# A routed feed-forward layer that sorts tokens into expert tiles through DRAM, and a shorter start of the delta attention

## The reference, cut to what matters

```python
def _L3_ffn_ref(x, Ws1, bs1, Ws2, bs2, We1, be1, We2, be2, Wr, br):
    D, E, HS, HR, TAU = 128, 12, 256, 384, 1.5
    xf = x.reshape(-1, Dm)                                   # 2048 tokens
    ys = _geglu(xf @ Ws1 + bs1) @ Ws2 + bs2                  # shared expert
    logits = (xf @ Wr + br) / TAU
    top_val, top_idx = jax.lax.top_k(logits, 2)
    top_w = jax.nn.softmax(top_val, axis=-1)
    onehot = jax.nn.one_hot(top_idx, E, dtype=x.dtype)
    w = jnp.einsum('nke,nk->ne', onehot, top_w)              # 2 of 12 nonzero
    act = _geglu(jnp.einsum('nd,edh->enh', xf, We1) + be1[:, None, :])
    yE = jnp.einsum('enh,ehd->end', act, We2) + be2[:, None, :]
    yr = jnp.einsum('end,ne->nd', yE, w)
    return (ys + yr).reshape(B, T, Dm)
```

## Time and profile before

| | |
|---|---|
| median of three runs | 3347.52 us (3342.79 to 3354.88) |
| the profiled execution's own time | 3348.08 us |
| its span in the profile | 3346.3 us, at a mean granted TensorE clock of 0.878 |
| busy: PE, DVE, ACT, POOL | 2732.6, 2249.3, 1317.0, 375.6 us |
| DMA | 213.99 MB, 64 GB/s on the mean |

### The profile page before, as it was taken

The page is one execution under the profiler, slowest core; times in us unless marked ns, Lnnn a source line. Parts: engine busy times, 40 slices in busy tenths (PEclk is TensorE's granted clock), DMA queues, the critical chain, the costliest instruction groups (busy, mean ns, idle before and its releaser), DMA issues. The chain is left out here.

```text
span 3346.3 us, 65597 instructions
## 1 busy us (share of the span) xinstructions
PE 2732.6 (82%) x25488; PEld 1777.4 (53%) x25488; DVE 2249.3 (67%) x3961; ACT 1317.0 (39%) x2809; POOL 375.6 (11%) x348
## 2 busy tenths in 40 slices
PE   6777887788778887799399999986775777699998
PEld 5677777777667776633166666632221222244443
DVE  4999999999999999700367778825665666422222
ACT  2233333333333333322367777741113454522223
POOL 0000000000000000000310110002330111044443
PEclk8788788788887778899699999997887899899999
DMA  4111111111111111110499999610001111211000
GB/s 157 27 28 27 27 28 27 27 27 27 27 27 27 27 27 27 36 25 0 109 228 243 238 230 248 158 47 2 0 0 41 46 43 37 96 36 31 31 31 31
DMA packets 194794, 213.99 MB, mean 64 GB/s; under 512 B 29842, under 2 KB 175650, under 8 KB 189138
## 3 DMA queue, kind: packets, MB, share of 16 engines
q1 hardware_dynamic: 194529, 210.03, 23.7%
HBM read 142.71 MB, written 67.03 MB: 63 GB/s over the span
## 5 line engine op out<-in xcount | busy, mean ns | idle before, releaser
L576 DVE SCALAR_TENSOR_TENSOR rf_A<-ps,rf_bias,rf_G 128x512 f32<-128x512 f32 x152 | 114.1, 751 | 275.2 <-POOL rf_G L558 260.6
L2364 DVE TENSOR_REDUCE dl_ZO<-dl_XP 128x64 f32<-128x128 f32 (+6 forms) x448 | 219.6, 490 | 15.4
L1104 DVE TENSOR_REDUCE ra_top<-ps 128x1 f32<-128x512 f32 x256 | 161.3, 683 | 94.7 <-PE ps L908 94.4
L547 ACT ACTIVATE rf_G<-ps,rf_bias 128x512 f32<-128x512 f32 x152 | 104.4, 687 | 287.8 <-PE ps L528 287.8
L558 POOL TENSOR_TENSOR rf_G<-rf_G,rf_WB 128x512 f32<-128x512 f32 x144 | 182.2, 1265 | 272.2 <-ACT rf_G L547 272.2
L2046 PE MATMUL ps<-dl_kqN,dl_ST 64*64 64x32 f32 x4224 | 195.3, 265 | 17.2 <-DVE dl_ST L2387 17.2
L2360 DVE TENSOR_TENSOR dl_XP<-dl_ZO,dl_G 128x64 f32<-128x64 f32 (+6 forms) x448 | 194.5, 434 | 15.4
L2046 PEld LDWEIGHTS ps<-dl_kqN,dl_ST 64*64 64x64 f32 x4224 | 192.5, 191 | 19.8 <-issue 19.7
L1303 POOL MEMSET da_K<- 32x4096 f32 x2 | 7.2, 3576 | 1607.6 <-POOLq L82 1607.6
L1758 DVE TENSOR_TENSOR ps<-ps,da_window 128x192 f32<-128x192 f32 (+1 forms) x256 | 101.2, 395 | 122.2 <-PE ps L1487 117.7
L1761 DVE TENSOR_REDUCE da_top<-ps 128x1 f32<-128x512 f32 x256 | 177.0, 691 | 8.8
(11 more groups left out here) (352 smaller groups left out, 6106.8 us busy)
## 6 DMA issues: line engine op xcount, KB each, us to landing
da_bands<-da_AB SPq DMA_DIRECT2D x128, 384.0 KB, 3.8
dl_Abc<-dl_ends SPq DMA_DIRECT2D x64, 512.0 KB, 6.2
da_window<-da_bands SPq DMA_DIRECT2D x128, 192.0 KB, 4.4
da_across<-da_bands SPq DMA_DIRECT2D x128, 192.0 KB, 4.4
rf_WB<-rf_shares SPq DMA_DIRECT2D x48, 256.0 KB, 3.2
da_parts<-da_split SPq DMA_DIRECT2D x64, 96.0 KB, 3.3
rf_We<-in_rf_We SPq DMA_DIRECT2D x1, 4608.0 KB, 15.9
da_K<-da_parts SPq DMA_DIRECT2D x16, 256.0 KB
```

Of the source, the lines that this page charges most:

```text
L1104: eng.tensor_reduce(top[:, m % 2, u:u + 1], ps[:, score_bank(UNITS * m + u), :], AXX, ALU.max, negate=True).then_inc(s["maxima"], 1)
L2364: link(eng.tensor_reduce(ZO[:, to:to + 1 + (2 * I - 1) * CH:CH].rearrange("p (k i) -> p k i", k=2), XP[:, :, :, SB - 1 - t:], AXX, ALU.add))
```

## The change

**Routed layer.** One block takes the place of two. After the top-2 chain, two matmuls with a strictly triangular matrix and with a matrix of ones count for each token how many tokens before it go to the same expert. DVE works these counts into a row number for each of the 4096 (token, choice) pairs: the rows of an expert are together and start at a multiple of 128. This gives SLOTS = 43 tiles of 128 rows (32 would hold 4096 rows; the rest is room for 12 experts that do not fill their last tile). The tiles run whether or not they hold rows.

- PE turns X into token-major tiles, ACT copies each of them twice to `XT`; a 129th column holds the row number to return to.
- SP fills all 43 x 128 rows of a DRAM array `rf_slots` with zeros and default row numbers (2.84 MB, rows of 516 B). POOL then **scatters** `XT` into it with 32 indirect DMAs of 128 rows. SP fetches it back in 11 DMAs of four tiles, one after the other.
- Meanwhile PE, ACT and DVE compute the shared expert and the term with be2 (28 matmuls of 512 columns) into R.
- **The tile loop**, written out 43 times: PE transposes the tile, DVE copies it to SBUF; DVE loads the tile's expert number into a register and copies the expert's first weights (128x768) to a fixed place `W1`, PE does 3 gate and 3 up matmuls of 128 columns, ACT 3 gelus, DVE 3 products, PE loads the same number into a register of its own and does 3 second matmuls with a register as address, ACT copies the result, POOL scatters it with an indirect DMA of 128 rows to the row (2 x token + choice) of `rf_results`.
- At the end SP loads the results of each batch (512 KB) one after the other, DVE weights and adds the two choices of each token, PE transposes the sum, DVE adds it to R.

**Delta layer.** PE starts the k projections as soon as the k taps are there, not those of q; the four `start(0, r)` on the zero state are left out, as is the transpose of `begin(0, 0)`, and `empty_state()` puts zeros and bv in place; DVE does both `prepare` before `gate_keys(0)`. The layer's semaphores are given back when the fifth layer begins, since the last layer needs 34.

The diff, cut to its core:

```diff
-            @block.sync
-            def _(eng):
-                eng.wait_ge(weights_c, B)
-                eng.dma_start(shares, WT[0:E, :, :]).then_inc(loaded, 16)
...
+        @block.sync
+        def _(eng):
+            eng.wait_ge(s["blank"], 1)
+            eng.wait_ge(s["marked"], 3)
+            eng.dma_start(slots.rearrange("(j p) x -> p j x", p=P), XS[:, :, :]).then_inc(s["filled"], 16)
+            eng.wait_ge(s["scattered"], 16 * 2 * NT)
+            for i, (first, last) in enumerate(FETCH):
+                if i:
+                    eng.wait_ge(s["fetched"], 16 * i)
+                eng.dma_start(XS[:, first:last, :], slots[first * P:last * P, :].rearrange("(j p) x -> p j x", p=P)).then_inc(s["fetched"], 16)
+            eng.wait_ge(s["returned"], 16 * SLOTS)
+            for b in range(B):
...
+                eng.dma_start(YT[:, span, :, :].rearrange("p t k x -> p t (k x)"),
+                              results[2 * b * T:2 * (b + 1) * T, :].rearrange("(t p k) x -> p t (k x)", p=P, k=2)).then_inc(s["gathered"], 16)
...
+        @block.gpsimd
+        def _(eng):
+            eng.memset(XS[:, :, 0:P], 0.0)
+            eng.memset(WT[:, :, :], 0.0).then_inc(s["blank"], 1)
+            eng.wait_ge(s["filled"], 16)
+            eng.wait_ge(s["x_copied"], 2 * B)
+            eng.wait_ge(s["marked"], 3)
+            eng.wait_ge(s["chain"], PLACED)
+            for k in range(2):
+                for t in range(NT):
+                    eng.indirect_dma_start(slots, bass.IndirectOffsetOnAxis(rows[:, k, t:t + 1], 0), XT[:, k, t, :], None)\
+                       .then_inc(s["scattered"], 16)
+            for j in range(SLOTS):
+                eng.wait_ge(s["fetched"], 16 * (j // 4 + 1))
+                eng.wait_ge(s["kept"], j + 1)
+                eng.indirect_dma_start(results, bass.IndirectOffsetOnAxis(XS[:, j, P:ROW].bitcast(U32), 0), Y[:, j, :], None)\
+                   .then_inc(s["returned"], 16)
...
+        @block.tensor
+        def _(eng):
...
+            def first(j):
+                eng.wait_ge(s["taken"], j + 1)
+                eng.wait_ge(s["brought"], j + 1)
+                if j >= 2:
+                    eng.wait_ge(s["tile_gelus"], j - 1)
+                    eng.wait_ge(s["tile_acts"], j - 1)
+                for m in range(HR):
+                    mm = eng.matmul(ps[:, 2 + j % 2, m * P:(m + 1) * P], W1[:, j % 2, (HR + m) * P:(HR + m + 1) * P], x[:, j % 3, :],
                                     start=True, stop=True)
+                mm.then_inc(s["gates"], 1)
...
+            def second(j):
+                e = eng.value_load(owners[0:1, j:j + 1], min_val=0, max_val=E - 1)
+                eng.wait_ge(s["tile_acts"], j + 1)
+                if j >= 2:
+                    eng.wait_ge(s["kept"], j - 1)
+                for m in range(HR):
+                    mm = eng.matmul(ps[:, 6 + j % 2, 0:P], A[:, j % 2, m, :], We2[:, bass.ds(e * (HR * P) + m * P, P)],
+                                    start=m == 0, stop=m == HR - 1)
+                mm.then_inc(s["outs"], 1)
...
+            for j in range(SLOTS):
+                if j + 2 < SLOTS:
+                    turn(j + 2)
+                if j + 1 < SLOTS:
+                    first(j + 1)
+                second(j)
...
+        @block.scalar
...
+            eng.wait_ge(s["chain"], OFFSET)
+            gelu(0)
+            for j in range(SLOTS):
+                if j + 1 < SLOTS:
+                    gelu(j + 1)
+                eng.wait_ge(s["outs"], j + 1)
+                eng.activation(Y[:, j, :], ps[:, 6 + j % 2, 0:P], ACT.Copy).then_inc(s["kept"], 1)
 
         @block.vector
...
+            step(eng.tensor_tensor(picked, passed[:, :, :].unsqueeze(2).to_broadcast([P, SLOTS, 2 * HR, E]),
+                                   own_bias.unsqueeze(1).to_broadcast([P, SLOTS, 2 * HR, E]), ALU.mult))
+            step(eng.tensor_reduce(offset[:, :, :], picked, AXX, ALU.add))
...
+            def bring(j):
+                e = eng.value_load(owners[0:1, j:j + 1], min_val=0, max_val=E - 1)
+                if j >= 2:
+                    eng.wait_ge(s["ups"], j - 1)
+                eng.tensor_copy(W1[:, j % 2, :], We1[:, bass.ds(e * (2 * HR * P), 2 * HR * P)]).then_inc(s["brought"], 1)
...
+            for j in range(SLOTS):
+                eng.wait_ge(s["ups"], j + 1)
+                eng.wait_ge(s["tile_gelus"], j + 1)
+                if j >= 2:
+                    eng.wait_ge(s["outs"], j - 1)
+                for m in range(HR):
+                    ins = eng.scalar_tensor_tensor(A[:, j % 2, m, :], ps[:, 4 + j % 2, m * P:(m + 1) * P], offset[:, j, m:m + 1], G[:, j % 2, m, :],
+                                                   ALU.add, ALU.mult)
+                ins.then_inc(s["tile_acts"], 1)
+                if j + 2 < SLOTS:
+                    bring(j + 2)
+                    take(j + 2)
...
             project(0, 2, 4, False)
+            eng.wait_ge(s["prepared"], 3)
+            project(0, 4, 6, False)
             eng.wait_ge(s["prepared"], 4)
-            project(0, 4, PROJ, False)
+            project(0, 6, PROJ, False)
...
-            for r in range(GR):
-                start(0, r)
+            eng.sem_inc(s["y"], GR)
...
+            def empty_state():
+                eng.memset(Y[:, CH:, :], 0.0).then_inc(s["begun"], 1)
+                eng.memset(XP[:, 1, :, 0:SB], 0.0).then_inc(s["begun"], 1)
+                eng.tensor_copy(XP[:, 0, :, 1:][:, :, ::-1], bv[:, 0, :, 0:SB]).then_inc(s["chain"], 1)
...
-            eng.wait_ge(s["prepared"], 4)
...
-            gate_keys(0)
             prepare(0, 0)
             prepare(0, 1)
-            begin(0, 0)
+            empty_state()
+            eng.wait_ge(s["prepared"], 4)
+            gate_keys(0)
             one_pass(0, True)
```

More of the change, by code:

```diff
@@ L487, in routed_ffn @@
-        experts = [(HR, E > 0)] * E + [(HS, False)]
-        before = [sum(h for h, _ in experts[:e]) for e in range(E + 2)]
-        HB = before[E + 1]
-        FREE = HR + 1
+        each = c.sb("rf_each", [P, E, NT], ctx)
+        upto = c.sb("rf_upto", [P, E, NT], ctx)
+        over = c.sb("rf_over", [P, E, NT], ctx)
+        count = c.sb("rf_count", [P, E], ctx)
+        ends = c.sb("rf_ends", [P, E], ctx)
+        begins = c.sb("rf_begins", [P, E], ctx)
+        place = c.sb("rf_place", [P, E, NT], ctx)
@@ new lines, in _ @@
+            eng.wait_ge(s["chain"], ROUTED)
+            flat = both[:, :, :].rearrange("p t e -> p (t e)")
+            eng.matmul(ps[:, 5, 0:NT * E], below[:, :], flat, start=True, stop=True)
+            eng.matmul(ps[:, 6, 0:NT * E], everyone[:, :], flat, start=True, stop=True).then_inc(s["prefixes"], 1)
+            eng.wait_ge(s["chain"], ROUTED + 2)
+            eng.wait_ge(s["x_copied"], 2 * B)
+            for t in range(NT):
+                mm = eng.transpose(ps[0:E, 1 + t // 4, (t % 4) * P:(t % 4 + 1) * P], weights[:, t, :], c.ident[:, :])
+                if t % 4 == 3:
+                    mm.then_inc(s["weights_turned"], 1)
@@ new lines, in _ @@
+            eng.wait_ge(s["weights_copied"], B)
+            eng.wait_ge(s["chain"], PLACED)
+            shared_first(0)
+            for b in range(B):
+                if b + 1 < B:
+                    shared_first(b + 1)
+                shared_second(b)
+            eng.wait_ge(s["base"], B)
+            eng.wait_ge(s["experts_loaded"], 16 * len(large))
+            eng.wait_ge(s["chain"], NAMED)
+            turn(0)
+            turn(1)
+            first(0)
+            for j in range(SLOTS):
[4 more added lines that the diff above has]
+                second(j)
@@ new lines, in _ @@
+            assert steps[0] == PLACED
+            per_slot = [P, SLOTS, E]
+            step(eng.tensor_tensor(passed[:, :, :], numbers[:, :].unsqueeze(2).to_broadcast(per_slot),
+                                   ends[:, :].unsqueeze(1).to_broadcast(per_slot), ALU.is_ge))
+            step(eng.tensor_reduce(owner[:, :], passed[:, :, :], AXX, ALU.add))
+            step(eng.tensor_scalar(owner[:, :], owner[:, :], float(E - 1), None, ALU.min))
+            step(eng.tensor_copy(owners[:, :], owner[:, :]))
@@ L583, in rwkv_attention @@
+            for b in range(B):
+                eng.wait_ge(s["back"], b + 1)
+                eng.tensor_tensor(c.R[:, b, :], c.R[:, b, :], ps[:, b, :], ALU.add)
 def rwkv_attention(c):
```

368 lines of the change are left out of this document (224 added, 144 removed).

## The result

The changed kernel takes 3100.46 us, the median of four runs (3093.74 to 3108.88), against 3350.18 for the kernel before in the same comparison: a ratio of 0.926, interval 0.923 to 0.929. The prediction said 3167 (3085 to 3275). The sign and the range held; the gain is 250 us where 181 were forecast.

The account below looks back on a forecast made before the run. TensorE's columns were taken to bound the last layer's loop, a waiting chain the delta prologue. Gains of 159 us in the last layer and 22 in the first took 3348.1 to 3167 us; range 3085 to 3275, with 0.8 inside.

Parts of the forecast that it names:

- the forecast as described: Whole kernel: the main case without the rivals, a total of 3110 to 3205 us, chance 0.54.
- the tile loop's 3.5 us a tile: Last layer's tile loop: 43 turns of 3.5 us, 150 us in all, bounds 2.5 and 5.5 a tile.
- PE 2.3: Tile loop: nine matmuls of 128 columns and a transpose take TensorE 2.3 us a tile at full clock.
- DVE 2.8, with 1 us for the register load: Tile loop: DVE's products and copies 1.7 to 2.2 us, plus a partly hidden 1 us register load, 2.8 a tile.
- 2.3 / 0.76 is 3.0, and PE's own load and semaphores come on it: Tile loop: TensorE's 2.3 us divided by the recurrence's granted clock, plus load and semaphores, taken as 3.5 a tile.
- the chain over two tiles: Tile loop: gates, gelus, products, load and copy, take and six hand-overs, 5.0 us over two tiles, 2.5 a tile.
- The half clock: Rival, PE in the tile loop: TensorE at 1.2 GHz, 5 us a tile, total 3210 to 3232, chance 0.13.
- The rival of slow ones: Rival, POOL's queue: slow indirect DMAs, total crossing 3348 at 5.1 us each, 3419 at 6; chance 0.11 for slower.
- its middle case: POOL's queue: an indirect DMA between 3 and 4.5 us, total 3215 to 3306, still faster; chance 0.11.
- 2.15 us each: Scatter: if all of a GpSimd DMA held POOL, 32 take 69 us and the total is 21 us more.
- 14 and 2 of landing: Fill of the slots: 14 us behind the large loads plus 2 of landing, so the scatter starts at 2935.
- All cheap: Rival, last layer: indirect DMA 0.45 us, register load 0.3, loop from 2963 at 2.5 a tile, total 3097, chance 0.08.

Follow-up runs that it names:

- run 7: Changed kernel with each register load of the tile loop done three times, on DVE and on PE: 3136.29 us, ratio 0.9355.
- run 4: Changed kernel with no register loads in the tile loop, every tile taking expert 0's weights by fixed addresses: 3100.19 us, ratio 0.927.
- run 6: Changed kernel with two more DVE copies of 128x512 in each turn of the tile loop, into an unread buffer: 3103.13 us, ratio 0.9273.
- run 8: Changed kernel with 32 more indirect DMAs of 64 rows each ahead of the scatter, POOL waiting for them: 3138.63 us, ratio 0.9387.
- run 9: Changed kernel with the two large weight loads issued after the fill on the same queue: 3104.51 us, ratio 0.9263.
- run 11: Changed kernel with each partition of the fill writing one contiguous run of 22 KB: 3093.53 us, ratio 0.9246.
- run 12: Changed kernel with large weight loads after the fill, four result loads issued at once, and the fill in long runs: 3087.68 us, ratio 0.9221.
- Run 10: Changed kernel with large weight loads after the fill and the four result loads issued at once, a semaphore each: 3096.11 us, ratio 0.9233.
- Run 3: Kernel before with only the k projections' earlier start, waiting for the k taps alone: 3342.76 us, ratio 0.9968.
- run 1: Kernel before with the whole delta layer part of the change alone: 3332.64 us against 3352.65, ratio 0.9939.

## Why the prediction was right, and where its sizes were off

**The mechanism held.** TensorE's columns bounded the last layer, the change takes them away, and none of the new costs is as large. The profiled pair gained 239 us where 181 were forecast. The last layer's terms, each beside the forecast of the section before (what lies between two events, us):

| | forecast | measured |
|---|---|---|
| first matmul to the scatter's start | 31 | 30.2 |
| 32 indirect DMAs | 48 | 40.4 |
| last landing, first fetch, first tile | 7.5 | 4.3 |
| tile loop with its end | 152 | 95.8 |
| tail | 26 | 22.5 |
| the layer | 265 | 193.3 |

Some 56 of the 72 us between the last two numbers are the tile loop. That the range held owes something to luck: 3100.46 is below the 3110 to 3205 of the forecast as described, and 3085 stood as the lower end only for a rival whose conditions were not met.

**The step that failed is the tile loop's 3.5 us a tile**; it is 2.10. Its working had three parts. *PE 2.3*: right, 2.10 measured. *DVE 2.8, with 1 us for the register load*: wrong. The load costs 0.4 us (run 7) and, in front of a copy that has time, nothing (run 4). DVE's busy time is 63.6 of 86 us, 1.55 a turn. *Then "2.3 / 0.76 is 3.0, and PE's own load and semaphores come on it"*: wrong, and the larger error. The clock of 0.76 came from a stretch of another make, where TensorE stands still for 3.70 us for one result of DVE's chain, and for 0.6 to 0.9 us at three other places. In the tile loop, after its first 7 us, TensorE waits for nothing and has 1.00; and run 7 has 1.00 even with a gap in each turn, so the division by 0.76 had no ground here. I had priced TensorE, DVE and the chain over two tiles each at 2.3 to 2.8 and then added a surcharge for their being close; run 6 shows DVE at 96% busy and the turn at 2.13. Being close to the bound cost little in this loop, where DVE prepares two tiles ahead (that this is the reason was not tried).

**The half clock** (0.13) fell as a state of the loop. Only its start shows it: after 17.7 us of standstill the six records of a gate group take 1.49 us at 2972.70 and 0.83 from 2976.03 on, and the stretch from 2968.9 to 2978 has 0.65. That costs some 2.5 us once (an estimate: four groups of six records, each 0.6 us longer from start to start than the later ones). From 2978 the loop has 1.00, as forecast against this rival, and in run 7, where TensorE pauses in each turn and is busy 80%, it is still 1.00. The rule of the Trainium skill on HAM oscillation ("TensorE: Matmul & The Clock Gate", section "HAM oscillation — how this bites in real kernels") did not bear on this loop: its case is a kernel that waits for a DMA in each turn, and its advice is on the number of output rows, not on every loop of 128-wide tiles with waits. No turn here waits for a DMA. In the same kernel the clock does fall elsewhere: 0.58 while the scatter alone works, 0.55 in the tail.

**The indirect DMA.** 1.5 us was taken from POOL's pass over 128 rows, 1.27; it is 1.26 with the gap, so the nearest row was nearer than what was added to it, and the term came out 7.6 us too high. That row is a product of 128x512 elements, and an indirect DMA is priced by the instruction (run 8), so that the two agree is luck. The rival of slow ones needed 5.1 us and fell with its middle case. The estimate from the page "DMA: Bandwidth & Descriptors" of the Trainium skill, 2.15 us each, fell as a time on POOL; a landing 2.3 us after issue is what the DMA issues of the changed kernel give for them, so its 2.0 us fixed, which the page puts down mostly to completion, are latency that the next one does not wait for.

**Routing and fill** came out within 1 us, the fill not for the reasons given. The row numbers were ready at +20.4 where "about 2923.5" was +19.5; its own terms (31 steps at 0.39 and 1.4 us of matmuls from 2911.1) add up to 2924.6, +20.6. The large loads landed at 2908, +14 (+15 forecast), and the fill 16 us after them, the number of "14 and 2 of landing". But it did not wait for them as priced: issued at 2900.57, it took 23.4 us beside them, and run 9, with no large load ahead of it, has 21.7. The price by packets, 22 us, was the right one for the whole fill, and starting beside the loads made up for it. The product over 3096 elements was priced 3.3 us and took 5.77. It was hidden beside the scatter, but not harmless: runs 11 and 12 show it in the way of whatever comes earlier.

**The shared expert** ended at 2952.1, +58 (+57 forecast), hidden beside the scatter.

**The tail** was four times 4.5 and is four times 3.6 to 3.9, in a chain as described; the loads land 3.7 us after issue. Run 10 shows that 5.4 us of it are the waits of the loads for each other.

**The delta layer.** First step 55.87 where 55.3 was forecast; products of keys end at 53.1 (52.4), both `prepare` at 49.5 (49.0), q starts at 40.26, not 39.70. Run 3 splits the 21.5 us: 10.9 for the earlier k (77.35 to 66.47), the rest for DVE's order and the state left out. Not foreseen: the gain shrinks to 17.8 at the last group of steps and to 11.6 at the layer's end in the profiled pair; 6.1 of what was lost lies in the last stretch with its lower clock. By the medians of run 1 it is 20, within the bounds of 17 to 23.

**"All cheap", 3097** (0.08), has nearly the measured total but not by its conditions: its indirect DMA was 0.45 us (1.26), its loop would have begun when the shared expert ended, at 2963 (the scatter still sets it), and its turn was 2.5 (2.10). Only its register load, 0.3, was near (0.4). Its errors cancel.

## What to carry to other kernels

Do not divide a new loop's matmul time by a granted clock that comes from a stretch of another make: price the loop at full clock first, and keep the lower clock as a rival. Do not add a surcharge only because several engines are close to the bound: here it was 1.2 us a turn that did not come. A few us in one trace prove nothing for an edit: the scatter's start, with the same fill, lay between +28.4 and +32.9. Scatter and gather through DRAM is priced by the number of indirect DMAs, so give each all 128 rows; write default rows in long runs (3.1 us of the layer here), and look at what large instructions with two inputs DVE has where GpSimd's DMAs are to start.

## What was not expected of the hardware

- **Packets.** The fill writes 2773.5 KB in packets of 516 B. After the weights have landed it runs at 140 GB/s (the stretch from 2908 to 2924). With no large load ahead of it, it takes 21.7 us (run 9), and in runs of 22 KB the same bytes take 8.9 (run 12).
- **VectorE and GpSimd seem to hold each other up**, in both directions. At the start of the changed layer DVE's copies of 16 and 43 elements to a partition take 6.3 us and end with POOL's two memsets (5504 and 2048 elements, 2893.96 to 2900.39; seen in the trace, not tried by itself), and in runs 11 and 12 one indirect DMA of 0.96 us takes 5.2 to 5.5 and ends 0.8 us after DVE's product.
- **A register load** of a value that has long been there costs an engine's list 0.4 us (run 7), and the loop nothing where the engine has time (run 4).
- **The granted clock** stayed at 1.00 with TensorE busy 80% in a regular loop, while the delta layer's last stretch had 0.63 in one execution and 0.73 in another for the same work. What decides between those two was not found.
